# A gated delta-rule layer in an eight-layer kernel: taps moved to ScalarE and VectorE, the gate network split and its logits transposed

## The reference

```python
q = silu(causal_dwconv(x @ Wq, conv_q)); k, v likewise        # 4 taps for each channel
beta = sigmoid(x @ Wb)
delta = delta_rule_chunkwise(q, k, v, beta)
f_short, f_long = fir(v, fir_short), fir(v, fir_long)
stats = concat([stats(f_short), stats(f_long), stats(delta), stats(v)])   # mean, var, mean|x|, norm per head
h1 = gelu(concat([x, stats]) @ W1 + b1)                       # once for each of 4 heads
p = softmax((h1 @ W2 + b2 + base_bias) / temp)                # 4 sources
p = maximum(p, [.05, .05, 0, 0]); p = p / sum(p)
o = p0*f_short + p1*f_long + p2*delta + p3*v + 0.5*sigmoid(residual)*f_short
out = rmsnorm(o, rms_w).reshape(B, L, H*DV) @ Wo
```

## Time and profile before

| | |
|---|---|
| median of 3 runs | 5954.96 us (5954.07 to 5967.87) |
| profiled execution, its own time | 5910.87 us |
| its span, first to last instruction | 5909.1 us |
| mean granted TensorE clock, whole span | 0.831 |
| `delta_inputs` stage | 4231 to 4527 us of the span |
| `gated_sum` stage | 5126 to 5728 us of the span |

### The profile page before, as it was taken

One profiled execution on the slowest core, in us unless ns is written; L12 is line 12 of the kernel. 1 busy time (PEld: TensorE's weight loads), 2 busy tenths in 40 slices (PEclk: granted clock), 3 DMA queues, 4 the chain that ended last, 5 costly groups with the idle time before them and its releaser, 6 DMA issues. The chain is left out here.

```text
span 5909.1 us, 188673 instructions
## 1 busy us (share of the span) xinstructions
PE 4521.7 (77%) x73798; PEld 2667.6 (45%) x73798; DVE 3079.9 (52%) x7440; ACT 2328.9 (39%) x4455; POOL 1820.8 (31%) x2634
## 2 busy tenths in 40 slices
PE   3888887374499999963819999995598999787855
PEld 1333333264255555553702333333366988644434
DVE  4555554433466656643437777774422553256654
ACT  0444445042255545522404666665332332123323
POOL 2333333213455555504042222210112332033321
PEclk9888789587699999966957999998798999855557
DMA  2111110211000000011111111110011112500001
GB/s 63 44 39 44 39 44 23 78 52 52 13 2 2 2 2 2 2 30 48 52 44 44 40 44 42 44 37 2 7 49 61 42 43 78 161 7 7 9 3 29
DMA packets 248212, 210.85 MB, mean 36 GB/s; under 512 B 62931, under 2 KB 220564, under 8 KB 247830
## 3 DMA queue, kind: packets, MB, share of 16 engines
q1 hardware_dynamic: 239638, 188.60, 10.5%
q0 software_dynamic: 8192, 16.79, 1.0%
HBM read 135.84 MB, written 68.94 MB: 35 GB/s over the span
## 5 line engine op out<-in xcount | busy, mean ns | idle before, releaser
L691 DVE TENSOR_REDUCE l_M<-l_max_bank 128x1 f32<-128x512 f32 (+3 forms) x2048 | 1101.1, 584 | 687.3 <-PE l_max_bank L494 433.2
L650 ACT ACTIVATE l_probs<-l_exp_bank 128x1024 f32<-128x1024 f32 (+3 forms) x1024 | 876.3, 864 | 789.2 <-PE l_exp_bank L509 774.2
L488 PE MATMUL l_max_bank<-l_KS,l_QS 48*128 48x512 bf16 (+3 forms) x2048 | 644.1, 374 | 214.5 <-DVE l_M L691 153.5
L473 PE MATMUL l_out_bank<-l_probs,l_V 128*32 128x256 f32 (+2 forms) x6144 | 550.4, 438 | 29.6 <-ACT l_heads_out L608 16.5
L509 PE MATMUL l_exp_bank<-l_QS,l_KS 49*128 49x512 bf16 (+3 forms) x2048 | 471.3, 366 | 13.8 <-ACT l_probs L650 13.7
L488 PEld LDWEIGHTS l_max_bank<-l_KS,l_QS 48*128 48x128 bf16 x2048 | 165.9, 96 | 684.2 <-DVE l_M L691 566.0
L390 POOL TENSOR_SCALAR_AFFINE_SELECT l_probs<-l_probs 128x256 f32<-128x256 f32 x512 | 206.7, 407 | 610.6 <-ACT l_probs L650 600.3
L1809 DVE TENSOR_REDUCE l_M<-l_max_bank 128x4 f32<-128x512 f32 x256 | 175.6, 686 | 171.1 <-PE l_max_bank L1628 171.1
L874 POOL DMA_INDIRECT l_back<-main_sorted_out,l_index x128 | 122.0, 953 | 413.5 <-issue 413.5
L1469 POOL TENSOR_TENSOR l_rms<-l_rms,l_minus_half 128x20 f32<-128x20 f32 x64 | 226.1, 3532 | 12.4 <-POOL l_rms L1466 12.4
L431 POOL TENSOR_TENSOR l_qk<-l_qk,l_cos 128x512 f32<-128x512 f32 x32 | 40.7, 1271 | 602.6 <-ACT l_rot L626 602.6
(11 more groups left out here) (415 smaller groups left out, 10789.2 us busy)
## 6 DMA issues: line engine op xcount, KB each, us to landing
l_parts_dram<-l_parts SPq DMA_DIRECT2D x64, 384.0 KB, 2.5
l_fir_band<-in_dr_short_dram SPq DMA_DIRECT2D x16, 1024.0 KB, 5.4
l_fir_band<-in_dr_long_dram SPq DMA_DIRECT2D x16, 1024.0 KB, 7.8
l_QS<-l_parts_dram SPq DMA_DIRECT2D x128, 96.0 KB
l_KS<-l_parts_dram SPq DMA_DIRECT2D x128, 96.0 KB
l_kqv_dram<-l_in_out SPq DMA_DIRECT2D x16, 768.0 KB, 3.4
l_core_ring<-l_kqv_dram SPq DMA_DIRECT2D x48, 256.0 KB, 3.4
l_rows<-main_sorted_in SPq DMA_DIRECT2D x152, 64.0 KB, 1.8
```

Source lines behind the costliest of these rows:

```text
L473: last = nc.tensor.matmul(out_bank[STRIP * h:STRIP * (h + 1), q0:q1], V[:, par, kb, 4 * j + h, :], probs[:, 2 * kb + h // 2, h % 2, q0:q1] ...
L488: return nc.tensor.matmul(max_bank[:, g, 0:W[t]], QS[64 * g:64 * g + ROWS, to, i, t * P:(t + 1) * P], KS[64 * g:64 * g + ROWS, to, i, 0:W[ ...
L650: nc.scalar.activation(probs[:, n, :, Q0[kb]:T], exp_bank[:, u % 2, :, Q0[kb]:T], ACT.Exp, scale=float(D) ** -0.5).then_inc(exp_done, 1)
L691: nc.vector.reduce_max(M[:, j % 2, col:col + 1], max_bank[:, g, 0:W[t]], AX.X)\
```

## The change

In `delta_inputs` the taps are no longer folded in. `project` is one 128x512 product of the plain weights. ScalarE copies the bank to `conv`, scaled by the newest tap (three copies for a sequence); VectorE adds the three older taps to it from the same bank, shifted by one to three tokens (`convolve`, nine instructions); only then does ScalarE apply Silu. `hT` is also stored to HBM (`hT_dram`).

In `gated_sum` that stored `hT` is loaded, so `hn`, its transposes and its copy go. The four 128-row products of the network stand together ahead of the wait for the statistics (`begin`), the four 16-row ones after it. The logits are four products with `w2`, padded to 32 columns, as weights, each in a 32-row strip of `logit_bank`; ScalarE copies them, and four transposes bring them to `stat_bank`. `rms_w` is multiplied into `wo` once. The sum over sources is two additions. The sums of b+2 are split and moved: those of the filters ahead of the wait for GpSimd's part, the others ahead of the wait for the root. The residual add of b moves to the list of b+1, behind its variances.

```diff
@@ delta_inputs
             def project(o, b, x):
-                for j in range(TAPS):
-                    last = nc.tensor.matmul(o, taps[:, j, x * C:(x + 1) * C], hT[:, b % 3, j:j + T], start=(j == 0),
-                                            stop=(j == TAPS - 1))
-                return last
+                return nc.tensor.matmul(o, w[:, x * C:(x + 1) * C], hT[:, b % 3, :], start=True, stop=True)
...
                 pe.wait_ge(hT_ready, b + 1)
                 if b:
-                    pe.wait_ge(kq_kept, b)
+                    pe.wait_ge(tapped, (b - 1) * 9 + 8)
                 project(kq_bank[:, 0, :], b, 1)
                 project(kq_bank[:, 1, :], b, 0).then_inc(kq_done, 1)
                 if b:
                     sums(b - 1)
-                    pe.wait_ge(v_kept, b)
+                    pe.wait_ge(tapped, b * 9)
                 project(v_bank[:, :], b, 2).then_inc(v_done, 1)
...
                 act.wait_ge(kq_done, b + 1)
+                if b:
+                    act.wait_ge(v_kept, b)
+                for x in range(2):
+                    nc.scalar.activation(conv[:, x, :], kq_bank[:, x, :], ACT.Copy, scale=taps[:, 1 - x, TAPS - 1:])\
+                      .then_inc(newest, 1)
+                act.wait_ge(v_done, b + 1)
+                nc.scalar.activation(conv[:, 2, :], v_bank[:, :], ACT.Copy, scale=taps[:, 2, TAPS - 1:])\
+                  .then_inc(newest, 1)
+                act.wait_ge(tapped, b * 9 + 8)
                 if b >= 3:
                     act.wait_ge(out_ready, b - 2)
-                nc.scalar.activation(kq[:, n, :, :], kq_bank[:, :, :], ACT.Silu).then_inc(kq_kept, 1)
-                act.wait_ge(v_done, b + 1)
-                nc.scalar.activation(vT[:, n, :], v_bank[:, :], ACT.Silu).then_inc(v_kept, 1)
+                nc.scalar.activation(kq[:, n, :, :], conv[:, 0:2, :], ACT.Silu).then_inc(kq_kept, 1)
+                act.wait_ge(tapped, b * 9 + 9)
+                nc.scalar.activation(vT[:, n, :], conv[:, 2, :], ACT.Silu).then_inc(v_kept, 1)
...
+            def convolve(b):
+
+                for j in range(TAPS - 1):
+                    back = TAPS - 1 - j
+                    for n, (row, bank) in enumerate(((1, kq_bank[:, 0, :]), (0, kq_bank[:, 1, :]), (2, v_bank[:, :]))):
+                        if j == 0:
+                            dve.wait_ge(newest, b * 3 + n + 1)
+                        else:
+                            dve.wait_ge(tapped, b * 9 + 3 * j + n - 2)
+                        v.scalar_tensor_tensor(conv[:, n, back:], bank[:, 0:T - back], taps[:, row, j:j + 1],
+                                               conv[:, n, back:], ALU.mult, ALU.add).then_inc(tapped, 1)
...
                     normalise(b + 2)
+                convolve(b)
                 if b:
                     invert(b - 1)
@@ gated_sum, SyncE
+            def load_next(b, n):
+                sp.wait_ge(shared, b + 1)
+                sp.dma_start(delta[:, n, :, :], delta_dram[bass.ds(b + 2, 1)]
+                             .rearrange("o (t p) c -> p (o t) c", p=P)).then_inc(delta_in[n], 16)
+                sp.wait_ge(hidden_begun, b + 1)
+                sp.dma_start(hT[:, n, :], hT_dram[bass.ds(b + 2, 1)].rearrange("o p t -> p (o t)")).then_inc(hT_in[n], 16)
@@ gated_sum, TensorE
+            def begin(b, half, n, first=False):
+
+                pe.wait_ge(hT_in[n], half * 16 + 16)
+                if not first:
+                    pe.wait_ge(gelu_done, b * DH)
+                for h in range(DH):
+                    last = nc.tensor.matmul(hidden_bank[:, h, :], w1[:, :], hT[:, n, :], start=True, stop=False,
+                                            skip_group_check=True)
+                last.then_inc(hidden_begun, 1)
...
                 for h in range(DH):
                     rows = slice(DK * h, DK * h + SOURCES * KINDS)
-                    nc.tensor.matmul(hidden_bank[:, h, :], w1[:, :], hT[:, :], start=True, stop=False)
-                    nc.tensor.matmul(hidden_bank[:, h, :], w1_stats[rows, :], statT[rows, :], start=False, stop=True)\
-                      .then_inc(hidden_done, 1)
+                    nc.tensor.matmul(hidden_bank[:, h, :], w1_stats[rows, :], statT[rows, :], start=False, stop=True,
+                                     skip_group_check=True).then_inc(hidden_done, 1)
                 if not first:
-
-                    pe.wait_ge(soft_step, b * SOFT_STEPS + (1 - SOFT_STEPS))
+                    pe.wait_ge(logitsT_kept, b)
                 for h in range(DH):
                     pe.wait_ge(gelu_done, b * DH + (h + 1))
-                    for t in range(TPS):
-                        c = (t * DH + h) * SOURCES
-                        last = nc.tensor.matmul(logit_bank[:, c:c + SOURCES], hidden[:, h, t * P:(t + 1) * P],
-                                                w2[:, :], start=True, stop=True)
+                    last = nc.tensor.matmul(logit_bank[DK * h:DK * h + DK, :], w2[:, :], hidden[:, h, :], start=True,
+                                            stop=True)
+                last.then_inc(logitsT_done, 1)
+                pe.wait_ge(logitsT_kept, b + 1)
+                for t in range(TPS):
+                    last = nc.tensor.transpose(stat_bank[:, t * P:(t + 1) * P], logitsT[:, t * P:(t + 1) * P],
+                                               identity[:, :])
                 last.then_inc(logits_done, 1)
@@ gated_sum, VectorE, the list of one sequence
+                if before:
+                    add(b - 1)
                 dve.wait_ge(exp_ready, b + 1)
...
                 share_out(v, sources(b, n)[0]).then_inc(filters_shared, 1)
+                if after == 2:
+                    sum_filters(b + 2, n)
                 dve.wait_ge(shared, b + 1)
                 dve.wait_ge(filters_shared, b + 1)
-                v.reduce_sum(o[:, :, :], weighted[:, :, :, :].rearrange("p s n d -> p n d s"), AX.X)\
-                 .then_inc(o_ready, 1)
+                v.tensor_tensor(weighted[:, 0:2, :, :], weighted[:, 0:2, :, :], weighted[:, 2:4, :, :], ALU.add)\
+                 .then_inc(o_step, 1)
+                dve.wait_ge(o_step, b + 1)
+                v.tensor_tensor(o[:, :, :], weighted[:, 0, :, :], weighted[:, 1, :, :], ALU.add).then_inc(o_ready, 1)
...
                 v.reduce_sum(rms[:, :], o_sq[:, :, :], AX.X).then_inc(ms_ready, 1)
+                if after == 2:
+                    sum_others(b + 2, half + 1, n)
                 dve.wait_ge(rms_ready, b + 1)
                 v.tensor_tensor(on[:, :, :], o[:, :, :], rms[:, :].unsqueeze(2).to_broadcast([P, TH, DK]), ALU.mult)\
-                 .then_inc(on_step, 1)
-                if follow == 2:
-                    sums(b + 2, n, i + 1)
-                dve.wait_ge(y_done, b + 1)
-                x = X[:, bass.ds(b * TPS, TPS), :].rearrange("p t c -> p (t c)")
-                v.tensor_tensor(x, x, y_bank[:, :], ALU.add).then_inc(added, 1)
+                 .then_inc(on_ready, 1)
```

More of the change, by code:

```diff
@@ L1892, in delta_inputs @@
         stored = [s.sem(f"stored{n}") for n in range(2)]
-        LOADED, MADE = 16 * 3, 6
+        hT_stored = [s.sem(f"hT_stored{n}") for n in range(3)]
+        LOADED, MADE = 16 * 3, 4
         block = s.block()
@@ L1984, in _ @@
             pe.wait_ge(made, MADE)
+            pe.wait_ge(loaded, LOADED)
             turn(0)
@@ L2641, in centre, with body @@
                 last.then_inc(centred, 1)
-            def body(i, b, n, follow):
-                m = (n + 1) % 2
-                if follow:
-                    centre(b + 1, m)
+            def body(b, half, n, after, before):
+                if after:
+                    centre(b + 1, (n + 1) % 2)
                 pool.wait_ge(shares_ready, b + 1)
@@ L2714, in body @@
                 last.then_inc(y_done, 1)
-            network(0, 0, True)
+            begin(0, 0, 0, first=True)
+            network(0, 0, first=True)
             sequences(body, pe)
@@ L2743, in network, with body @@
                       .then_inc(gelu_done, 1)
-            def body(i, b, n, follow):
-                if follow:
+                act.wait_ge(logitsT_done, b + 1)
+                nc.scalar.activation(logitsT[:, :], logit_bank[:, :], ACT.Copy).then_inc(logitsT_kept, 1)
+            def body(b, half, n, after, before):
+                if after:
                     square(b + 1)
@@ L2769, in _, with sum_up @@
             v.tensor_scalar(log_temp[:, :], log_temp[:, :], 0.0, 1e-4, ALU.max, ALU.add).then_inc(made, 1)
-            dve.wait_ge(made, 5)
+            dve.wait_ge(made, 6)
             v.tensor_tensor(inv_temp[:, :], log_temp[:, :], soft[:, :], ALU.add).then_inc(made, 1)
-            dve.wait_ge(made, 6)
+            dve.wait_ge(made, 7)
             v.reciprocal(inv_temp[:, :], inv_temp[:, :]).then_inc(made, 1)
+            v.tensor_scalar(wo[:, :], wo[:, :], rms_w[:, 0:1], None, ALU.mult).then_inc(made, 1)
             dve.wait_ge(made, MADE)
-            def sums(b, n, i):
```

(10 more changed lines are left out.)

142 lines of the change are left out of this document (82 added, 60 removed).

## The result

The changed kernel takes 5736.9 us (median of four runs, 5731.8 to 5742.1) where the kernel before takes 5954.5 (5948.9 to 5967.9) beside it. The ratio is 0.9639, 95% interval 0.9621 to 0.9658: 217.6 us, or 3.6%, less. The forecast was 5787, 168 less, with a range of 5715 to 5850.

The account below looks back on a forecast made before the run. TensorE was taken to bound both stages; the change would save 198 us in `gated_sum` and cost 30 in `delta_inputs`, so 5954.96 - 168 = 5787 us. The range was 5715 to 5850, the forecast's own 5765 to 5815.

Parts of the forecast that it names:

- The loop sum of 22.7: `gated_sum`: new period through GpSimd, ScalarE and VectorE, 22.0 plus 0.7 for interference, down from 34.8 us.
- tie: `gated_sum`, shares to additions: VectorE's own share and filter sums, 3.6 us, called equal to GpSimd's two weighted sources, 3.2.
- The sum for TensorE's loop, 22.7 at half clock: `gated_sum`: TensorE's path from `begin` (8.0) through 16-row products, Gelus, logits and transposes to output products, 22.7 us per sequence.
- rival 2: `gated_sum`: 16-row products stay serial or clock makes TensorE the bound; period 26.7 or 24.9, 5820 to 5847 us; chance 0.20.
- The 0.7 us that I added for `on` beside `centre`: `gated_sum`: interference allowance, as VectorE's `on` starts together with GpSimd's `centre`; 0.7 us per period.
- The 22.0 that I derived from it: `gated_sum`: GpSimd loop without interference, if `on` waits for a 1.99 us piece of `centre` and `centre` loses nothing.
- I take 19.0, near the cold end: `delta_inputs`: period of 19.0 us with k and q cold, `sums` and v partly; +31 us over 15 periods.
- full-clock sum of 14.7: `delta_inputs`: new loop of copies, taps, Silu, roots and TensorE's products at full clock, 14.7 us per sequence.
- half-clock sum: `delta_inputs`: the same loop with its four TensorE terms doubled, 20.3 us per sequence, the +49 us bound.
- Rival 1: `delta_inputs`: the clock holds, 14.7 us per sequence, total 5722 us; chance 0.17.
- Rival 3: `delta_inputs`: Silu's table load (1.28) falls behind the taps at cold clock; 21.6 per sequence, +69, 5826 us; chance 0.10.
- Rival 4: `delta_inputs`: shifted taps read the bank badly; slower once each costs 2.3 us instead of 0.68, 5986 at 2.7; chance 0.03.

Follow-up runs that it names:

- on_first: Changed kernel, but GpSimd centres the next sequence's residual only after VectorE has made `on`; 5737.3 us, `gated_sum` 422.8 us against 414.2.
- one_reduction: Changed kernel with the old single reduction over four weighted sources in place of two additions; 5758.8 us, `gated_sum` 441.4 us.
- logits_narrow: Changed kernel with the old 16 narrow logit products in place of four wide ones, their copy and transposes; 5741.0 us, `gated_sum` 415.3 us.
- same_strip: Changed kernel, but all four 16-row products read rows 0 to 15 instead of four row strips; 5734.3 us, `gated_sum` 417.1 us.
- interleaved: Changed kernel with `begin` undone, each head's 128-row product again right ahead of its 16-row one; 5848.8 us, `gated_sum` 530.4 us.
- busy1: Changed kernel with the 12 spreading products of `delta_inputs` made twice to fill TensorE's pause; 5722.6 us, `delta_inputs` 268.4 us.
- root_act: Changed kernel with the root of the mean square on ScalarE and its reciprocal on VectorE, instead of GpSimd's power; 5731.9 us, `gated_sum` 403.2 us.

## Why the prediction was right, and by how much it was off

The forecast was 5787 and the time is 5736.9. It lies outside the forecast's own range of 5765 to 5815, and inside the wider one only because that one was drawn to take in rivals which didn't happen. What was right is the larger part, `gated_sum`; `delta_inputs` was forecast the wrong way.

**gated_sum, -198 forecast, -207.0 measured.** The mechanism held, all but one leg. The periods gave -189.1 for -181, the start -16.5 for -14.1 (-15.6 and the loads' +1.5), the end -1.4 for -3. The loop sum of 22.7 is a period of 22.3 in steady state: `centre` 4.5 for 4.1, squares 1.9, variances 2.9, the residual add 0.6 for 0.7, shares 2.15 for 2.2, from the shares to the additions 3.4 for 3.2, additions to mean square 3.4 for 3.3, root and handovers 3.3 for 3.4. The leg of 3.4 was put down to GpSimd's weights and is VectorE's own work, the side of that "tie" (3.6 against 3.2) that I left out of the sum. `on_first` and `one_reduction` show by their prices (+8.6 and +27.2) that this loop sets the time.

**What I had tied and wasn't.** The sum for TensorE's loop, 22.7 at half clock, was off: TensorE waits 6.5 us per sequence. `begin` took 5.1 for 8.0. Part of that is no matter of clock: I priced a product in it at the 2.0 us of the alternating ones, where four in a row cost 0.86 a record even at half clock, 6.9 in all, the price that rival 2 uses. The rest, and the 16-row products' 1.14 for 2.1, come from the clock, which rises within `begin`, at a place where it never rose before. With that slack, `logits_narrow` (+1.1) and `same_strip` (+2.9) cost next to nothing, and rival 2 needs both the clock and the slack gone, as in `interleaved` (28.9 for its 26.7). Its lower bound was mis-summed: 26.7 less 8 x 0.3 is 24.3, not 24.9, some 9 us less in all.

**Interference.** The 0.7 us that I added for `on` beside `centre` was put on the wrong instruction. `on` took 2.44 for 0.69, and two softmax products 0.85 and 0.74 for 0.22, all of it while GpSimd's pieces ran; `centre`'s first piece was as long as ever (1.97), its second lost 0.45. The Trainium skill (SBUF — State Buffer, SBUF: two separate sides) has this right, and its reading, which I weighed and left out of the sum, was the better one: `on` blocked for about a whole piece of `centre`. Only that `centre` would lose nothing, which I drew from it, was wrong: its second piece in turn stood behind `on`. The 22.0 that I derived from it is 0.3 under the period, and 22.7 is 0.4 over.

**delta_inputs, +30 forecast, -7.4 measured. The step that failed in size is the term "I take 19.0, near the cold end".** The period is 17.07. K and q cold in every sequence was right (3.62 for the 3.4 named), and so was the pause (4.15 for 5). Adding only what they and their transposes lose at half clock, 1.7 and 0.5, to the full-clock sum of 14.7 gives 16.9; the forecast added 4.3. But `sums` and v run at full clock behind them: v takes 1.10, and the sums 2.8 from 4419.01, where I had them partly cold. Of the +31, the 13 full gaps should have had 27 and had 1; the last two, which drain the loop, 4 and had -3. The full-clock sum of 14.7 stands: `busy1` has periods of 14.78. The taps were 0.74 for 0.68 and the scaled copies 0.69 for 0.60. (The half-clock sum is 20.4, not 20.3; the bound hardly moves.) At the start I counted 1.8 for the folding of the taps; 7.5 came. What I left out is the load of the taps, 3.7 us less to wait for, and the first turns, from the first product to the first copy of v, 28.0 us before and 25.7 after: nine products less, and the taps added.

Together the miss is 50 us: 37 in `delta_inputs`, 9 in `gated_sum`, and 3 that can't be placed. No rival took place. Rival 1's 5722 is nearer the time than the forecast is, but not by its mechanism: the clock fell to 0.70. Rival 3's order did not come about; Silu's table load (1.28) lies beside the taps. Rival 4's taps would have had to cost 2.3.

## What to carry to other kernels

When TensorE's work is taken out of a stage, sum the loop that doesn't touch TensorE first: here it gave 22.7 for 22.3, and the wide logits, which only shortened TensorE further, were worth nothing. Undoing `begin` alone cost 116 of the 207 us, the two additions 27. Read which products run cold behind a pause and price only those: here k, q and their transposes, not `sums` and v. Count the first and last turns of a loop apart, and with them the first loads. Behind a wait that is removed look for the work it covered: here VectorE's sums stood 0.4 us behind GpSimd's root. Moving the root alone gave 11 us of the stage, and moving also the part of `centre` that depended on neither gave 19 more.

## What the runs showed of the hardware that was not expected

- 128-row and 16-row products in turn, 16.0 us of them and TensorE never idle: granted clock 0.50 (1.2 GHz) for all of them, in the kernel before as in `interleaved`. Four 128-row ones together: 0.50 in the first 2.5 us and 0.89 in the mean of the next 2.4, so 2.4 GHz in most of that. What in the alternation holds it down was not separated (row count or weight loads).
- Twelve useless products in a pause made a stage 20 us shorter (288.5 to 268.4), and three of 13 gaps stayed at 17.05 to 17.07 all the same.
- A VectorE product over 64 elements a partition went from 0.22 to 1.73 us beside GpSimd's `centre` (in `root_act`), and 0.85 in the changed kernel.
- GpSimd's power over 128 x 16 takes 2.90 us, ScalarE's square root of the same 0.31 and VectorE's reciprocal 0.25; the table load that comes with it (1.28) was hidden.
